# Who reads the cleared-region count in the counting stage, and which load the first strip waits for

## What is computed

```python
def _gcn_conv(x, W, b, src, dst, norm, num_nodes):
    h = x @ W
    msg = h[src] * norm[:, None]
    out = jax.ops.segment_sum(msg, dst, num_segments=num_nodes)
    return out + b
...
h = jax.nn.relu(_gcn_conv(x, W1, b1, src, dst, norm, num_nodes))
h = jax.nn.relu(_gcn_conv(h, W2, b2, src, dst, norm, num_nodes))
out = _gcn_conv(h, W3, b3, src, dst, norm, num_nodes)
return out + x
```

## Time and profile before

| what | us |
|---|---|
| median of 3 runs | 7734.77 (7733.99 to 7738.77) |
| the profiled execution, its own time | 7740.96 |
| its span in the trace | 7739.1 |
| PE busy in the span | 6070.4 (78%) |
| DVE busy | 4467.4 (58%) |
| ACT busy | 3018.7 (39%) |
| matmuls of the counting stage, L2169, busy | 742.4 |
| matmuls of the convolutions, L2288, busy | 1039.0 and 519.5 |

### The profile page before, as it was taken

The page is one execution under the profiler, slowest core; times in us unless marked ns, Lnnn a source line. Parts: engine busy times, 40 slices in busy tenths (PEclk is TensorE's granted clock), DMA queues, the critical chain, the costliest instruction groups (busy, mean ns, idle before and its releaser), DMA issues. The chain is left out here.

```text
span 7739.1 us, 133599 instructions
## 1 busy us (share of the span) xinstructions
PE 6070.4 (78%) x34928; PEld 4272.6 (55%) x34928; DVE 4467.4 (58%) x13848; ACT 3018.7 (39%) x8075; POOL 4040.9 (52%) x4041
## 2 busy tenths in 40 slices
PE   6757627789957288775666556899999699999999
PEld 4326416788833144333555444899999444444444
DVE  9987915566644799776666666788888400000000
ACT  0001103444502136776666664788888100000000
POOL 6777777777677777502777771677777000000000
PEclk9877869999969699998777787999999899999999
DMA  1003312222230135665222224999999488788787
GB/s 46 3 6 95 98 50 55 55 55 55 50 99 13 29 95 178 202 213 158 53 53 53 53 52 126 364 383 386 379 382 381 181 294 293 284 294 293 290 304 266
DMA packets 531654, 1300.21 MB, mean 168 GB/s; under 512 B 107301, under 2 KB 332697, under 8 KB 498442
## 3 DMA queue, kind: packets, MB, share of 16 engines
q0 software_dynamic: 221568, 548.08, 22.0%
q1 hardware_dynamic: 114942, 568.32, 20.6%
q10 hardware_dynamic: 194700, 178.41, 7.1%
HBM read 1066.26 MB, written 228.24 MB: 167 GB/s over the span
## 5 line engine op out<-in xcount | busy, mean ns | idle before, releaser
L1979 PE MATMUL edge_p_m<-edge_rows,edge_onehot 128*128 128x128 f32 x9984 | 1128.8, 276 | 42.1 <-ACT edge_rows L1911 36.9
L1979 PEld LDWEIGHTS edge_p_m<-edge_rows,edge_onehot 128*128 128x128 f32 x9984 | 1120.5, 192 | 50.3 <-issue 28.7
L201 POOL DMA_INDIRECT edge_rows<-tab,edge_slots x832 | 811.9, 976 | 635.8 <-DMA edge_slots<-slots_s 382.4
L201 POOL DMA_INDIRECT edge_rows<-tab,pairs_pair_src x832 | 838.9, 1008 | 490.8 <-issue 218.9
L2288 PE MATMUL conv_p_o<-conv_ring,acc_acc 128*128 128x512 f32 (+1 forms) x2548 | 1039.0, 569 | 31.6 <-DMA conv_roots<-dis_row 31.2
L1911 ACT ACTIVATE edge_rows<-edge_rows,edge_coef 128x128 f32<-128x128 f32 x3328 | 995.5, 387 | 168.7 <-DMA edge_rows<-tab,pairs_pair_src 168.7
L2169 PE MATMUL adj_cells<-adj_hot_joint,adj_hot_low 128*128 128x392 bf16 x3920 | 742.4, 332 | 354.0 <-SPq L2115 255.1
L208 POOL DMA_INDIRECT slots_s<-source_pays,source_row_s x782 | 842.9, 1078 | 286.7 <-issue 250.9
L577 POOL DMA_INDIRECT slots_d<-all_slots,pro_row_d x782 | 763.7, 977 | 295.0 <-issue 247.0
L982 POOL DMA_INDIRECT all_x<-tab_src,all_slots x784 | 744.3, 949 | 254.0 <-issue 238.8
L2288 PEld LDWEIGHTS conv_p_o<-conv_ring,acc_acc 128*128 128x128 f32 x2548 | 468.3, 191 | 585.0 <-issue 553.6
(11 more groups left out here) (457 smaller groups left out, 10041.3 us busy)
## 6 DMA issues: line engine op xcount, KB each, us to landing
conv_ring<-adjacency SPq DMA_DIRECT2D x252, 1792.0 KB, 7.1
adjacency<-adj_counts ACTq DMA_DIRECT2D x196, 784.0 KB
tab<-tab_o SPq DMA_DIRECT2D x50, 512.0 KB, 2.6
edge_rows<-tab,edge_slots POOLq DMA_INDIRECT x832, 2.6
edge_rows<-tab,pairs_pair_src POOLq DMA_INDIRECT x832, 5.9
tab_src<-all_x SPq DMA_DIRECT2D x50, 260.0 KB
tab_dst<-acc_acc SPq DMA_DIRECT2D x50, 260.0 KB
acc_acc<-tab_dst SPq DMA_DIRECT2D x50, 260.0 KB
```

The costliest lines, as they stand in the source:

```text
L201: pool.indirect_dma_start(out=rows[:, slot, j, :], out_offset=None, in_=table[:, :], in_offset=bass.IndirectOffsetOnAxis(ap=index, axis=0) ...
L1979: m = pe.matmul(at, onehot[:, z, j, :], rows[:, slot, j, b * H:(b + 1) * H], start=(n == 0), stop=(n == len(PARTS) - 1))
```

## The change

In the counting stage SP's relay loop and its two semaphores are gone. For every second pair PE now loads the needed count into a register of its own and waits for `half_cleared`, and ahead of the third matmul for `cleared`, directly against that register. In the convolution the loads count on three semaphores (`bias_in`, `roots_in`, and `loaded` for the four of weights and biases): DVE waits for `last_bias` ahead of its two additions and for `roots` behind them, ACT for the weights and biases, and PE waits for those only after its second strip.

```diff
         @block.sync
         def _(sp):
             sp.dma_start(offset[:, :], D["negoff"]).then_inc(q["loaded"], 16)
-            for k in range(VT // 2):
-                buckets = sp.value_load(regs[REG_SP:REG_SP + 1, ALLOWED + k:ALLOWED + k + 1], min_val=1, max_val=REAL + 1)
-                sp.wait_ge(q["half_cleared"], buckets)
-                sp.sem_inc(q["half_allowed"], 1)
-                sp.wait_ge(q["cleared"], buckets)
-                sp.sem_inc(q["allowed"], 1)
...
                     if n % 2 == 0:
-                        pe.wait_ge(q["half_allowed"], n // 2 + 1)
+                        ready = pe.value_load(regs[REG_SP:REG_SP + 1, ALLOWED + n // 2:ALLOWED + n // 2 + 1], min_val=1, max_val=REAL + 1)
+                        pe.wait_ge(q["half_cleared"], ready)
                     pe.wait_ge(q["hot"], n + 1)
                     for c in range(4):
                         if n % 2 == 0 and c == 2:
-                            pe.wait_ge(q["allowed"], n // 2 + 1)
+                            pe.wait_ge(q["cleared"], ready)
...
-            act.dma_start(last_bias[:, :], A["L3_gnn_b3"].rearrange("(a h) -> a h", a=1).to_broadcast([P, H])).then_inc(q["loaded"], 16)
+            act.dma_start(last_bias[:, :], A["L3_gnn_b3"].rearrange("(a h) -> a h", a=1).to_broadcast([P, H])).then_inc(q["bias_in"], 16)
...
-            act.dma_start(roots[:, :], D["dis_row"][0:HI, :].rearrange("(a w) p -> a (w p)", a=1).to_broadcast([P, HI * P])).then_inc(q["loaded"], 16)
-            act.wait_ge(q["loaded"], 16 * 6)
+            act.dma_start(roots[:, :], D["dis_row"][0:HI, :].rearrange("(a w) p -> a (w p)", a=1).to_broadcast([P, HI * P])).then_inc(q["roots_in"], 16)
+            act.wait_ge(q["loaded"], 16 * 4)
...
-            v.wait_ge(q["loaded"], 16 * 6)
+            v.wait_ge(q["bias_in"], 16)
...
             v.wait_ge(q["added"], 2)
+            v.wait_ge(q["roots_in"], 16)
...
-            pe.wait_ge(q["loaded"], 16 * 6)
             for layer in range(LAYERS):
                 for k in range(STRIPS):
                     strip(layer, k)
+                    if layer == 0 and k == 1:
+                        pe.wait_ge(q["loaded"], 16 * 4)
                     if k:
                         turn(layer, k - 1)
```

More of the change, by code:

```diff
@@ L2097, in build_adjacency @@
         cells = s.ps("cells", [P, 2, 4, 512])
-        q = {n: s.sem(n) for n in ("loaded", "dve", "emptied", "hot", "allowed", "product", "taken", "cleared", "half_cleared", "half_allowed")}
+        q = {n: s.sem(n) for n in ("loaded", "dve", "emptied", "hot", "product", "taken", "cleared", "half_cleared")}
         stored = [s.sem(f"stored{z}") for z in range(STAGES)]
@@ L2207, in convolve @@
         p_y = s.ps("p_y", [P, 2, 512])
-        q = {n: s.sem(n) for n in ("loaded", "added", "freed", "summed", "scaled", "rectified", "turned", "rows_done", "stored")}
+        q = {n: s.sem(n) for n in ("loaded", "bias_in", "roots_in", "added", "freed", "summed", "scaled", "rectified", "turned", "rows_done", "stored")}
         arrived = [s.sem(f"arrived{z}") for z in range(A_RING)]
```

## The result

The changed kernel takes 7948.87 us (median of 4 runs, 7942.09 to 7953.26) against 7736.77 us (4 runs, 7733.99 to 7746.94): a ratio of 1.0275, with a 95% interval of 1.0262 to 1.0288. It is 212 us slower, the forecast was 7913. Its profiled execution has a span of 7945.0 us, 205.9 more than before.

A forecast was written before the change was run, and what follows sets the result against it. PE in the convolution ends last, but stages run one after another, so the counting stage's loss counts fully. +199 - 21 = +178 us on 7740.96 gives 7919; the median stands 6.2 under, so 7913, range 7825 to 7990.

The forecast's parts named there:

- The direction and the mechanism: Counting stage: added load chains are exposed on PE's sequencer and PE takes the lead from DVE; slower, 0.86.
- The price of a group: Counting stage: PE needs 4.22 us for a group with short loads, 0.6 us for each added chain.
- The long loads: Counting stage: a long load adds 0.56 us; half of each stretch's DMA share taken as their share.
- The lower bound of 1066: Counting stage with no long load and today's 4.72 us as the last stretch's floor: 1066 us, +126.
- The sum: Whole kernel: +199 for the counting stage, -21 for the first strip, +178 us in all; median 7913 us.
- The relay: Counting stage: removing SP's relay counted as 0 us gain, bounded by 0 and 85 us.
- The first strip: Convolution's start: PE no longer waits for `roots` and starts 21 us earlier; 17 if earlier units starve.
- The rival in which it gains nothing: Convolution's start: ring and `roots` share DMA engines, the first unit comes later; 7934 us, chance 0.05.
- Hidden loads: Counting stage: chains hidden by PE's sequencer or existing waits, stage stays at 940; 7714 to 7629 us, chance 0.10.
- The boundary: Hidden-loads rival decides from about 0.2 us for a chain, where the first counting stretch takes 356 us, +16.
- The clock: Counting stage: gaps in PE's work lower its clock, a third of groups at 1.2 GHz; 8130 us, chance 0.05.
- Long loads that go with the relay: Counting stage: SP and PE reading together makes loads long; all short without relay, 7840 us, chance 0.15.

The follow-up runs named there:

- e3: The change with the added word loaded without bounds, a mask replacing FUSED_REGOPS and SEQ_ASSERT: 7872.4 us, ratio 1.0178; counting stage 1099.5 us.
- e4: The change without the added load, the needed count worked out on PE by two register operations: 7760.15 us, ratio 1.0032; counting stage 985.2 us.
- e6: The change with every chain of load and bounds made twice: 8349.4 us, ratio 1.0793; counting stage 1578.3 us.
- e8: The change without ACT's stores in the counting stage, zeros stored behind it; only the stage is read, 1085.6 us.
- e1: The kernel before with only the convolution's split loads, relay kept: 7716.19 us against 7733.49, ratio 0.9977; counting stage 941.9 us.
- e10: Relay kept, convolution's loads split, run once more on another chip: 7713.7 us, ratio 0.9978 to the kernel before; counting stage 941.4 us.
- e9: Relay of before with split convolution loads, SP's load moved between the relay's two waits: 7749.58 us, ratio 1.0026; counting stage 980.7 us.
- e7: The change without bounds, one two-word load per group instead of two one-word loads: 7823.43 us, ratio 1.0117; counting stage 1050.6 us.

## Why the prediction was right, point by point

**The direction and the mechanism hold.** PE's sequencer is the bound: e3, e4 and e6 change only what PE's sequencer has to do, and the stage follows in both directions, by 84, 198 and 395 us.

**The price of a group was too low.** The forecast had 4.22 us for a group with short loads. e8, where no load is long, takes 1085.6 / 245 = 4.43 us, which makes 52 us over the stage. A chain accounts for 22 of them: it takes 0.64 us and not 0.6, or 0.044 x 490. On PE the load takes 0.304 us (e8) against SP's 0.267, and its FUSED_REGOPS 0.151 against 0.147. The group's own load costs 0.39 us instead of 0.36, some 7 in all. What the other 23 are stays open. Where the miss lies can be said: in its first 104, next 77 and last 64 groups the change takes 4.60, 4.87 and 5.15 us for a group, where the forecast had 4.51, 4.74 and 4.77. So 24 of the 44 us between 1139 and 1183 are in the last part. There PE still waited for clears, 24 us in 24 places, which the forecast took to be covered by the chains; no run takes these waits away by themselves. The sentence of the prediction that nothing spoke for a slower sequencer on PE is the weak one: it compared four words on PE (0.334 us) with one on SP, and that comparison can't tell the engine from the number of words.

**The long loads cost about what was counted, in part by luck.** The forecast of 1139 us holds 105 us for them: 0.29, 0.53 and 0.55 us for a group in the three stretches. The stores turned out to be worth 98. The share of long loads was a guess, half of the DMA share, 26% in the mean; 201 of PE's 735 loads, 27%, took over 0.45 us. What sets the share is something else: whether a load starts in the part of the time behind a store's issue in which they are long. That it is the stores, which the forecast only guessed, is shown by e8. The lower bound of 1066 isn't the forecast less the long loads, since it has a floor of 4.72 us under the last stretch; e8 does the last 64 groups at 4.53, so without the stores there is no such floor.

**The sum.** The stage is 43 us over the forecast's 199, and the whole only 36 us over 7913. The stages that the change doesn't touch took 15 off, and the median of the runs lies 2 us over the profiled execution where the forecast took it 6 under. Neither was foreseen, so that the whole came nearer than the stage is chance.

**The relay gave nothing back.** With the load gone and the waits direct (e4) the stage is still 44 us over the one with the relay. Whatever the relay's absence won is less than what two register operations cost; in the last 64 groups, where PE waits for clears most, the two are equal.

**The first strip gave its 21 us** at its first matmul, and 20 after the first strip. e1 and e10 measure it as 17 us in the whole, with an interval of some 8 to either side. The rival in which it gains nothing falls.

**The rivals.** Hidden loads: PE did wait for clears in 54 places only, and 0.58 us for a load, read from two rows, said it already. The boundary that the prediction drew for it was too generous: it gave a chain of 0.2 us 16 us in the first stretch (21 were to be lost there), and e4's two operations of 0.19 us lost 35 in the same groups. The Trainium skill gives TensorE a queue 64 deep (TensorE: Matmul & The Clock Gate, the opening table), which would have hidden the chains if it had been full; the runs don't agree, since each chain of e6 cost 0.81 us. The floor of 600 ns for a tensor_load (the Trainium skill, DMA: Bandwidth & Descriptors, Latency and other measured facts) isn't borne out either: 0.304 us is the median in e8. The clock: 0.96 to 1.00 in the change, so it didn't come; in e6, with the chain twice, it fell to 0.81 and added next to nothing. Long loads that go with the relay: refuted, as the maximum of 0.907 us on PE without any load on SP in this stage shows.

**What was to be seen.** 1201 matmuls between 2660 and 3000 (some 1200 forecast), DVE at 73% (70%), pieces of 8, DVE's waits for PE 375 us (over 300). Two marks missed: the shortest load takes 0.299 us, not 0.26 to 0.29, and the stage lasts 1183 us, not 1140.

## What to carry to other kernels

A register load on an engine that issues many short instructions isn't free: here a load with bounds on PE cost 0.64 us of matmul time without stores (e8), and 0.81 with them (e6). An idle engine that did the load and answered with a constant to wait for was the cheaper place, even with a hop between. Before moving such a load, look at whether the engine's sequencer is ahead: the distance between the starts around an existing load shows it. And where a releaser in the trace had been done for microseconds, look for what the trace doesn't count as busy.

## What was not expected of the hardware

A TENSOR_LOAD of one word takes 0.26 to 0.32 us while nothing is stored, and up to 0.9 us behind the issue of ACT's store of a bucket. PE's, DVE's and ACT's loads are all from the same tile, and removing only the stores brought every one of PE's 490 under 0.32 us (e8). The long ones start in a part of the store's time only, 0.76 to 2.93 us after its issue in the change, while it lands after 3.8. So where a load stands against the store matters beside how many there are: put between the relay's two waits on SP, into the time after a store's issue, its median went from 0.272 to 0.523 us (e9). And two words in one load took longer, 0.54 us, than four, 0.336 (e7).
